# Head-masked state slots in a chunked state-space scan: one 32-row by 128-column product in place of two 32-row by 64-column ones

## The reference, cut to what matters

```python
def step(h, inp):
    x_t, B_t, C_t, dt_t = inp
    dA = jnp.exp(dt_t * A)[:, :, None, None]
    h = dA * h + dt_t[:, :, None, None] * x_t[..., None] * B_t[:, None, None, :]
    y_t = jnp.einsum('bhpn,bn->bhp', h, C_t) + D_param[None, :, None] * x_t
    return (h, y_t)
```

## Time and profile before

| | |
|---|---|
| median of 3 runs | 1075.17 us (1074.15 to 1076.78) |
| the profiled execution, its own time | 1074.0 us |
| its span in the trace | 1072.2 us |
| instructions in the trace | 29421 |
| TensorE products busy | 1021.1 us (95%) |
| VectorE busy | 935.9 us (87%) |
| ScalarE busy | 933.3 us (87%) |
| GpSimd busy | 489.9 us (46%) |

### The profile page before, as it was taken

One profiled execution on the slowest core, in us unless ns is written; L12 is line 12 of the kernel. 1 busy time (PEld: TensorE's weight loads), 2 busy tenths in 40 slices (PEclk: granted clock), 3 DMA queues, 4 the chain that ended last, 5 costly groups with the idle time before them and its releaser, 6 DMA issues.

```text
span 1072.2 us, 29421 instructions
## 1 busy us (share of the span) xinstructions
PE 1021.1 (95%) x11470; PEld 652.2 (61%) x11470; DVE 935.9 (87%) x1992; ACT 933.3 (87%) x1620; POOL 489.9 (46%) x590
## 2 busy tenths in 40 slices
PE   5759999999999999999999999999999999999996
PEld 3344757566675756667576665756667575665674
DVE  5999998989998999998989988998989899875666
ACT  4869598999989888999898999998999999978785
POOL 1445444543545435443644552455434425443733
PEclk9989999999999999999999999999999999999999
DMA  7423242555564554555455356545555553452658
GB/s 257 102 53 80 66 88 52 100 103 89 101 119 93 100 84 97 105 97 114 73 124 90 84 99 110 107 76 106 84 90 119 81 110 62 94 96 58 125 110 163
DMA packets 303659, 106.20 MB, mean 99 GB/s; under 512 B 271904, under 2 KB 299808, under 8 KB 303520
## 3 DMA queue, kind: packets, MB, share of 16 engines
q1 hardware_dynamic: 303520, 104.31, 49.3%
HBM read 28.38 MB, written 8.91 MB: 35 GB/s over the span
## 4 chain that ended last, share of the span: by engine, by line
PE 69%; DVE 14%; ACT 7%; issue 5%; DMA 3%; SPq 1%; POOL 1%; DVEq 0%; ACTq 0%; POOLq 0%
PE bank L413 41%; PE bank L673 8%; PE bank L685 7%; PE bank L613 3%; PE bank L594 2%; DVE cv L1081 2%; PE bank L622 2%; PE bank L519 2%; DVE sty L1214 1%; ACT L183 1%; DMA x<-in_x 1%; PE bank L568 1%; DVE yT L1206 1%; DVE st L1036 1%; DVE Xd L1143 1%
## 5 line engine op out<-in xcount | busy, mean ns | idle before, releaser
L413 PE MATMUL bank<-xnT,win 128*128 128x512 f16 x1152 | 275.5, 383 | 3.5 <-DVE th L1169 1.2
L183 ACT ACT_TABLE_LOAD x156 | 200.1, 1283 | 2.8
L413 PEld LDWEIGHTS bank<-xnT,win 128*128 128x128 f16 x1152 | 110.2, 99 | 121.7 <-issue 5.3
L413 PE MATMUL bank<-yhl,wg 128*128 128x512 f16 x768 | 176.5, 381 | 0.6 <-DMA yhl<-ynh 0.5
L1391 POOL TENSOR_TENSOR caty<-tg,caty 128x512 f16<-128x512 f32 x64 | 83.0, 1297 | 189.6 <-ACT caty L890 189.5
L1081 DVE SCALAR_TENSOR_TENSOR cv<-bank,cws,cv 128x511 f32<-128x511 f32 (+2 forms) x192 | 142.9, 746 | 6.4 <-ACT tail L790 1.4
L673 PE MATMUL bank<-wfc,x3T 128*128 128x512 f16 x512 | 130.0, 380 | 1.7 <-issue 1.3
L685 PE MATMUL bank<-wpj,hT 128*128 128x256 f16 x1024 | 122.4, 273 | 6.3 <-DMA hT<-hb 5.6
L413 PEld LDWEIGHTS bank<-yhl,wg 128*128 128x128 f16 x768 | 73.2, 98 | 87.5 <-issue 5.4
L1386 POOL TENSOR_TENSOR yT<-yhl 128x512 f32<-128x512 f16 x64 | 78.4, 1237 | 96.8 <-DMA yhl<-ynh 96.8
L1395 POOL TENSOR_TENSOR cat<-sz,cat 128x512 f16<-128x512 f32 x64 | 83.8, 1311 | 81.2 <-ACT cat L902 68.0
(11 more groups left out here) (167 smaller groups left out, 2037.8 us busy)
## 6 DMA issues: line engine op xcount, KB each, us to landing
x<-in_x SPq DMA_DIRECT2D x31, 512.0 KB, 4.6
out_y<-x SPq DMA_DIRECT2D x15, 512.0 KB, 3.2
crep<-c_rows SPq DMA_DIRECT2D x16, 256.0 KB
hT<-hb SPq DMA_TRANSPOSE x128, 3.3
caty<-in_wg SPq DMA_DIRECT2D x1, 1024.0 KB, 8.1
x<-in_wout SPq DMA_DIRECT2D x1, 1024.0 KB, 9.7
hT<-in_wfc SPq DMA_DIRECT2D x1, 1024.0 KB, 10.4
hb<-in_wpj SPq DMA_DIRECT2D x1, 1024.0 KB, 7.1
```

The lines of the kernel that those rows point to most:

```text
L183: self.eng.preload_act_table_set(self.table)
L413: m = eng.matmul(b, lhs(p, k), rhs(q, k), start=(n == 0), stop=(n == len(seq) - 1))
```

## The change

The slots of `S` now hold zeros where the state numbers of one head meet the channels of the other. A constant mask `smask` (128 x 128) is made at the start with two copies of 128 x 64. A new VectorE step `state_mask` (t, 16 of them, one for each block) multiplies what `states` left in the two banks by this mask and writes it into the 8 slots ahead. Each operation takes as many sub-chunks of one parity as lie in the ring before it wraps; so a block has 2, 3 or 4 of them, and the 16 blocks together have 53 (in order of the blocks 2, 2, 3, 4, 4, 4, 4, 4, 3, 2, 2, 3, 4, 4, 4, 4). The banks of `states` come free behind it (`s_zero`) and no longer behind `advance`, which reads the masked states from the slot that it then overwrites.

`c_grown` makes one decayed C with one operation of 128 x 512 without a head mask. The wait for its own completion now stands behind the copy into `dec`.

`carried` has one product for each sub-chunk and pair: weights 32 rows by 128 columns, 64 streamed columns, all 128 partitions written. That is 32 products for a block in place of 64, on 4 tiles (the 4 groups of rows) in place of 8. `ec` shrinks from 128 x 1024 to 128 x 512, and the tensor `smask` is new.

All five order strings are replaced. TensorE, ScalarE, GpSimd and the DMA queue have the same steps as before, at other places; VectorE's has the 16 steps t besides. Around block 7 VectorE's string goes from `e7 o5 q4 28 j4 x7 n6 i4 o5 48 c8 o5 x7 c8 p4 v6 X5 S7` to `e7 c8 c8 o5 V5 c8 v6 X5 48 t7 k6 p4 k6 q4 j4 S7`, and TensorE's from `t753 q746 G62 s80 v61 m83 p45 G62 q747 f56 G61 r74370` to `t735 G64 G60 v66 s81 q743 q750 p42 f54 G63 f56 G65 m80 z71 r77436`.

At the start of the kernel the DMA queue's string goes from `K0 W0 K0 W0 h0 W0 h1 h1 d0 c0 W0` to `W0 W0 K0 W0 h0 W0 K0 h1 h1 d0 c0`. The steps W load four weights of 1,024 KB in turn (gate, output, feed-forward in, feed-forward out), K loads the two halves of the constants that `dt_last` waits for, and h0 loads the input of block 1. VectorE's string goes from `W0 c0 a1 u0 N0 00 c0 20 c0 Z0 c0 40` to `N0 c0 a1 u0 00 20 c0 40`, where a1 is the variance of block 1, c a convolution's taps (three operations), and 4 `dt_last`, which writes `ahl`, the decays that TensorE's `cum` (m) needs.

The diff, with the order strings cut:

```diff
--- before.py
+++ after.py
@@ -30,131 +30,131 @@
         "Silu": "silu_and_others"}
 
 PE_ORDER = (
...
 )
 ACT_ORDER = (
...
     "mf jf qf jf "
 )
 DVE_ORDER = (
...
 )
 POOL_ORDER = (
...
 )
 SP_ORDER = (
...
     "je je Xf Xf Xf je je Xf je je jf jf jf jf pe jf jf jf jf pf pf pf pf "
 )
 
@@ -225,8 +225,8 @@
             sem(n) for n in "yn yf_ev y_hi tanh yg_hi z_silu cat_hi gelu h_mu h_sq hn_hi x2_hi".split())
         win_hi, an_exp, wg_hi, wout_hi, w_abs, bhl_hi = (sem(n) for n in "win_hi an_exp wg_hi wout_hi w_abs bhl_hi".split())
 
-        v_step, consts, x_var, xn_lo, taps, u_cp, dt_min, dt_one, a_hl, cum_rest, seg_l, xd, ce, be, gm = (
-            sem(n) for n in "v_step consts x_var xn_lo taps u_cp dt_min dt_one a_hl cum_rest seg_l xd ce be gm".split())
+        v_step, consts, x_var, xn_lo, taps, u_cp, dt_min, dt_one, a_hl, cum_rest, seg_l, xd, ce, be, gm, s_zero = (
+            sem(n) for n in "v_step consts x_var xn_lo taps u_cp dt_min dt_one a_hl cum_rest seg_l xd ce be gm s_zero".split())
         s_done, em, y_out, y_var, y_lo, yg, sx, x2_out, x2_var, x2_lo, hn, h_var, hn_lo, x_out = (
             sem(n) for n in "s_done em y_out y_var y_lo yg sx x2_out x2_var x2_lo hn h_var hn_lo x_out".split())
         win_lo, aneg_v, wg_lo, wout_lo, gam_v, wq, bhl_v, r0_v, bgh_v = (
@@ -283,7 +283,7 @@
         segR = sb("segR", [P, 2, 8, P], f16)
         segL = sb("segL", [P, 2, P], f16)
         pick = sb("pick", [P, NCH, 8, 16], f16)
-        ec = sb("ec", [P, 2, T])
+        ec = sb("ec", [P, T])
         dec = sb("dec", [P, 2 * NCH])
         yT = sb("yT", [P, 4, T])
         ynh = sb("ynh", [P, 2, 2, T], f16)
@@ -323,6 +323,7 @@
         esuf = sb("esuf", [P, NCH, 8])
         Gm = sb("Gm", [P, NCH, SUB])
         S = sb("S", [P, 9, P])
+        smask = sb("smask", [P, P])
         crep = sb("crep", [P, T])
         banks = [ctx.enter_context(nc.psum_tensor(f"bank{n}", [P, T], f32)) for n in range(8)]
 
@@ -569,8 +570,8 @@
                                            BE[rows(e), c, 2 * j:2 * j + 2, :].rearrange("p e n -> p (e n)"),
                                            Xd[rows(e), c, j * P:(j + 1) * P], start=True, stop=True)
                 m.then_inc(st_mm, 1)
-                gives(at0, s_done, i + 1)
-                gives(at1, s_done, i + 1)
+                gives(at0, s_zero, i + 1)
+                gives(at1, s_zero, i + 1)
 
             def seg(i, n, at0, at1):
                 hold = [take(at0), take(at1)]
@@ -589,11 +590,10 @@
                 pe.wait_ge(ce, i + 1)
                 pe.wait_ge(s_done, i + 1)
                 for k in range(2 * NCH):
-                    for e in range(2):
-                        for j in range(4):
-                            m = eng.matmul(hold[j][rows(e), sub(0, k)], S[32 * j:32 * j + 32, (8 * i + k) % 9, rows(e)],
-                                           ec[32 * j:32 * j + 32, e, sub(0, k)], start=(k == 0), stop=False,
-                                           skip_group_check=True)
+                    for j in range(4):
+                        m = eng.matmul(hold[j][:, sub(0, k)], S[32 * j:32 * j + 32, (8 * i + k) % 9, :],
+                                       ec[32 * j:32 * j + 32, sub(0, k)], start=(k == 0), stop=False,
+                                       skip_group_check=True)
                 m.then_inc(car_mm, 1)
                 for j in range(4):
                     gives(at[j], y_out, 4 * i + j + 1)
@@ -836,7 +836,7 @@
                 act.load("Exp")
                 act.wait_ge(ec_mm, i + 1)
                 act.wait_ge(car_mm, i)
-                eng.activation(ec[:, 0, :], b[:, :], ACT.Exp).then_inc(ec_exp, 1)
+                eng.activation(ec[:, :], b[:, :], ACT.Exp).then_inc(ec_exp, 1)
 
             def exp_s(i, n):
                 (b,) = bank["s", i, 0]
@@ -972,6 +972,9 @@
             eng.memset(none[:, :], 0.0)
             eng.memset(mone[:, :], -1.0)
             eng.memset(mhalf[:, :], -0.5)
+            dve.wait_ge(ld_const, 16)
+            for e in range(2):
+                eng.tensor_copy(smask[:, rows(e)], of_head[e].broadcast_to([P, SUB]))
             dve.wait_ge(ld_ul, 16)
             eng.tensor_copy(ul[:, :, :], ulf)
             dve.wait_ge(ld_small, 16)
@@ -1152,12 +1155,9 @@
             def c_grown(i, n):
                 dve.wait_ge(ec_exp, i + 1)
                 dve.wait_ge(s_done, i)
-                eng.tensor_copy(dec[:, :], ec[:, 0, :].rearrange("p (c t) -> p c t", t=SUB)[:, :, SUB - 1])
-                dve.wait_ge(ld_const, 16)
+                then(eng.tensor_copy(dec[:, :], ec[:, :].rearrange("p (c t) -> p c t", t=SUB)[:, :, SUB - 1]))
                 dve.wait_ge(rep, 16 * (i + 1))
-                then(eng.scalar_tensor_tensor(ec[:, 1, :], crep[:, :], of_head[1], ec[:, 0, :], ALU.mult, ALU.mult))
-                eng.scalar_tensor_tensor(ec[:, 0, :], crep[:, :], of_head[0], ec[:, 0, :], ALU.mult, ALU.mult
-                                         ).then_inc(ce, 1)
+                eng.tensor_tensor(ec[:, :], crep[:, :], ec[:, :], ALU.mult).then_inc(ce, 1)
 
             def b_suffix(i, n):
                 (b,) = bank["b", i, 0]
@@ -1178,16 +1178,31 @@
                     eng.tensor_tensor(Gm[:, 2 * p:2 * p + 2, :], b[:, 0:P].rearrange("p (c t) -> p c t", c=2),
                                       causal.unsqueeze(1).broadcast_to([P, 2, SUB]), ALU.mult).then_inc(gm, 1)
 
-            def advance(i, n):
+            def state_mask(i, n):
                 hold = bank["t", i, 0]
                 dve.wait_ge(st_mm, i + 1)
+                dve.wait_ge(s_done, i)
+                dve.wait_ge(car_mm, i)
+                for e in range(2):
+                    c = 0
+                    while c < NCH:
+                        to = (8 * i + 2 * c + e + 1) % 9
+                        m = min(NCH - c, (8 - to) // 2 + 1)
+                        op = eng.tensor_tensor(S[:, to:to + 2 * m - 1:2, :],
+                                               hold[e][:, c * P:(c + m) * P].rearrange("p (c f) -> p c f", f=P),
+                                               smask[:, :].unsqueeze(1).broadcast_to([P, m, P]), ALU.mult)
+                        c += m
+                op.then_inc(s_zero, 1)
+
+            def advance(i, n):
+                dve.wait_ge(s_zero, i + 1)
                 dve.wait_ge(ce, i + 1)
                 dve.wait_ge(s_done, i)
                 dve.wait_ge(car_mm, i)
                 for k in range(2 * NCH):
                     at = 8 * i + k
                     op = eng.scalar_tensor_tensor(S[:, (at + 1) % 9, :], S[:, at % 9, :], dec[:, k:k + 1],
-                                                  hold[k % 2][:, chunk(k // 2)], ALU.mult, ALU.add)
+                                                  S[:, (at + 1) % 9, :], ALU.mult, ALU.add)
                     if k < 7:
                         then(op)
                 op.then_inc(s_done, 1)
@@ -1288,7 +1303,7 @@
             STEPS = {"W": weights_in, "N": minus_a, "H": thresholds, "T": ternary,
                      "C": centre, "R": bias_out, "G": bias_gate, "a": var_x, "h": rest_x, "c": tap, "u": copy_u,
                      "0": dt_zero, "2": dt_plus, "4": dt_last, "5": cum_left, "6": cum_last, "x": x_dt, "Z": zero_s,
-                     "e": c_grown, "b": b_suffix, "g": gram_mask, "S": advance, "E": mix, "Y": y_rows,
+                     "e": c_grown, "b": b_suffix, "g": gram_mask, "t": state_mask, "S": advance, "E": mix, "Y": y_rows,
                      "y": var_y, "n": rest_y, "k": gate_y, "v": skip, "o": add_x, "X": rest_x2, "V": var_x2,
                      "i": centre_h, "q": var_h, "j": rest_h, "p": add_ffn}
             for letter, i, n, _ in steps_of(DVE_ORDER):
```

## The result

The changed kernel takes 1078.09 us (median of 20 runs, 1075.38 to 1081.85), the kernel before 1075.38 us (20 runs, 1073.06 to 1077.79): a ratio of 1.0022 [1.0014, 1.0030]. That is 2.7 us more, where the sum of the prediction had 8.1 (5.8 + 1.1 + 1.2). The time lies in the range and the direction is right. The size is a third of the forecast: the interval leaves out no change, but the difference stays inside the 0.3% (3.2 us) that the prediction called "same".

A forecast was written before the change was run, and what follows sets the result against it. TensorE was taken to bound nearly every block, VectorE the blocks starting in the first 110 us. Profiled 1074.0 + 5.8 (product) + 1.1 (VectorE) + 1.2 (order) = 1082.1 us, 1083.3 in the median's terms; range 1069 to 1090 us.

The forecast's parts named there:

- The loads don't hide: Rival at `carried`: 128-column weight loads hide, -7.0 us in place of +5.8, giving 1070.5 us; chance 0.19.
- the count of instructions within the stage doesn't decide: Rival at `carried`: half the instructions take half of 1.53 us, 12.2 us less, giving 1065.3 us; chance 0.03.
- the extra 27 ns of the narrow tile: Rival at `carried`: 32-row tiles keep 27 ns more a turn, 7.1 us over the forecast, 1090.4 us; chance 0.16.
- half the instructions stand on half the tiles: Product stage `carried`: still 16 turns a tile, at 109 ns each, 1.89 us a block, +5.8 us in 16 blocks.
- TensorE's idle time should stay near 6 us: Check on TensorE from 170 to 890 us: idle time stays near 6 us; over 4 us either way means wrong.
- +5.8: Product term at `carried`: 0.36 us more a block over 16 blocks, bounds -7.0 to +12.9 us.
- VectorE's +11.8 us "hidden" from 170 us on: VectorE: masks add 24.9 us, one C saves 13.0; hidden from 170 us on by 60.7 us of free time.
- the 1.1 us I gave them: VectorE term: 0.55 us more in each of blocks 0 and 1, where VectorE is the limit, +1.1 us.
- if the cover were gone everywhere, all 11.8 us would show: Upper case for VectorE's added work: with no free time hiding it in any block, 11.8 us.
- `advance` "costed at nothing": State step on VectorE: keeps 8 operations of 0.347 us, only the third operand comes from SBUF; no cost.
- the same steps stand at other places, so only idle time can change, +1.2 us: New order: at the start, block 1's input 2.9 us later, `ahl` 1.7 us sooner; +1.2 us, bounds -5.1 to +2.9.
- the new order pays for the loads: Rival: loads cost as forecast, but the order takes 6.1 us of TensorE's idle time, giving 1077.2 us; chance 0.16.

The follow-up runs named there:

- c_merged: The kernel before in its own order with only the one decayed C, 64 products, no masks, zeros left out: 1076.26 us, ratio 1.0005.
- full_old_order: The changed kernel with the order strings of before, each mask step right in front of its block's state step: 1108.67 us, 1.0302 of the kernel before.
- wide_unmasked: The kernel before in its own order with one decayed C and the 32 wide products, no masks, zeros left out: 1073.39 us, ratio 0.9976.
- zeros_in_b: The kernel before in its own order with wide products, one C, and zeros laid in B, `states` multiplying each head by itself, no masks: 1078.54 us, ratio 1.0028.
- halves_new_order: The changed kernel with 64 products of 64 columns a block again; masks, one C and new orders kept: 1086.8 us, 1.0102 of the kernel before.

## Why the prediction came out as it did

**Right.** The product stage is limited by the turns on a tile, and 128-column fp32 loads make a turn 112 ns; the estimate by the Trainium skill (TensorE: Matmul & The Clock Gate, section LDWEIGHTS) was 107. The loads don't hide, the count of instructions within the stage doesn't decide, and the extra 27 ns of the narrow tile did not stay; these three rivals are out. The masks' count and duration were right.

**Wrong, first step: "half the instructions stand on half the tiles"** priced the stage by its turns alone and gave the 2,048 instructions less (128 a block) no worth anywhere else. Before, the next packet of instructions came too late at some places: 5.4 us of gaps, 3.2 of them in the 6.1 us of idle time that I saw from 170 to 890 us and left standing as "TensorE's idle time should stay near 6 us". The changed kernel has 0.2 us. So +5.8 was really +6.7 less 5.2 for the gaps and some more for the stages around them; in the old order the exchange is -2.9 us, and there my sum had +5.8.

**Wrong, second step: VectorE's +11.8 us "hidden" from 170 us on.** In the old order masks, one C and moved operand cost 30 us against the 1.1 us I gave them, and the masks alone 20, so most of its 60.7 us of free time there was no cover for work put in front of S. Half a sentence, "if the cover were gone everywhere, all 11.8 us would show", was the right question with too low an answer. The sum also took the saved C operation at its full 0.8 us a block against the masks; in `c_merged` that saving was worth nothing.

**Wrong, third step: `advance` "costed at nothing".** Its 128 operations take 10.8 us more, since both big operands now come from SBUF while GpSimd works. In the old order, with the masks there, that is 12 us of time.

**Wrong, fourth step: "the same steps stand at other places, so only idle time can change", +1.2 us.** That the total at the start came out near is partly luck: TensorE has 1.1 us more of idle time in 110 us, where order and masks together were to cost 2.3, but by other parts. The wait for `ahl` is gone, with the decays at 29.6 us in place of 33.1, and the wait for the input, which was to grow from 2.6 to some 5 us, shrank to 0.8. And the order's worth was another: it gave back 30.6 us, by the starts of `carried` 6 us of them up to block 2 and 21 more up to block 15. It put work between `states`, masks and S and used the early banks. Behind TensorE's longer waits in the old order its clock was down as well: after the first 100 us some 24 us of `full_old_order` ran at 1.2 GHz, by my estimate at most 12 us of the 30.

That the sum still came within 5 us is luck, since the steps cancel: 1075.6 + 0.7 for one C (not apart from nothing by its interval) - 2.9 for the product is the 1073.4 us of `wide_unmasked`, and masks, moved operand and new order together leave 4.7 us, 1078.1 us. The rival "the new order pays for the loads" (1077.2 us) came nearest, by another sum: the order paid for the masks, and the refills for the loads. Not parted are the early banks, the placing of t and the clock within the 30.6 us, since the old code in the new order waits for other reasons. No kernel that computes the whole reference was measurably faster than before; the 2.2 us of `wide_unmasked` are there only as long as the zeros cost nothing.

## What to carry to other kernels

Look for idle time of an engine with "issue" in the midst of a run of identical small instructions, and compare its places with the instruction queue's packets: there the number of instructions has a price, and wider ones that take longer can still win. In a program with a fixed order, an engine's idle share is no cover until each gap is seen to lie behind the work that is added. Here work put on VectorE's way to the next product cost 20 of its 24 us, while 7 us taken off elsewhere on the same engine gave nothing; so set a high bound at the whole duration, and then ask what a new order gives back. When an operand moves from PSUM to SBUF, check what GpSimd does at that time. When a stall grows, look at the granted clock behind it.

## What the runs showed of the hardware

- TensorE's instructions come in packets of 16,384 bytes, some 252 to 255 products and loads. Where small ones follow each other fast, gaps of 0.2 to 2.7 us with nothing awaited appear; 52 of 56 in seven traces end 1.2 to 1.9 us after a packet has landed and stand at one place within a packet; a shift by half a packet moves them to other steps, one by a whole packet brings 6 of 9 back at the same ones. Bursts of 256 in 1.5 us also occur without a gap (`zeros_in_b`).
- Behind gaps of 1.9 and 2.35 us of TensorE in `halves_new_order` the granted clock was 1.2 GHz; in the changed kernel it stayed at 2.4 GHz from 100 us to the last product.
- A 128 x 128 fp32 VectorE operation with two operands in SBUF lasts 352 ns, and up to 1290 ns beside a GpSimd operation; with one of them in PSUM it never passed 349 ns in 128, 69 of which lay beside one in the kernel before.
- fp32 turns on a tile: 112 ns with 32 rows and 128 columns; a stage of 64 products of 64 rows, 32 columns and 64 streamed takes 1.50 us where 32 products with 128 streamed take 1.09.
